# Cross-attention and expert FFN in one kernel: the experts' weights split on ScalarE and GpSimd, the context's LayerNorm applied on GpSimd, and new orders of work on all five engines

## Chip, cores and metric

One core of a Trainium2 chip. The metric is the device time of one execution in microseconds; the time before is the median of three runs. A span is the time from the first to the last instruction of the profiled execution.

## What is computed

Inputs: x (4, 512, 128), a context (4, 77, 96) with a mask of its valid positions, weights of one attention and of eight experts. All in float32.

```
ln   = layernorm(layernorm(x)) * g + b              # latents: 4 x 512 x 128
xn   = layernorm(ctx) * g + b                       # context: 4 x 77 x 96
q    = ln @ Wq.T
k, v = concat(xn @ Wkv.T, ln @ Wlkv.T)              # 77 + 512 keys, 2 heads of 64
attn = softmax(rmsnorm(q) * 64**-0.5 @ rmsnorm(k).T, masked context keys out)
x    = x + (attn @ v) @ Wo.T + bo
l2   = layernorm(x)
gates = softmax(l2 @ Wg + bg); top 2 of 8 experts
x    = x + sum over the two chosen e: gate[e] * (l2 @ W[e] + b[e])
```

## The kernel before

Each batch's 512 rows are four tiles of 128. The front (LayerNorm, q, k, v, their norms) runs over five parts p: batch 0 in two halves (parts 0 and 1), then batches 1, 2, 3 (parts 2, 3, 4). The rear (scores, exp, values, denominators, projection, second LayerNorm, gate, experts) runs over four parts, the batches. Per batch there are five groups of keys (four of 128, the context as the fifth): `score p n` is six matmuls for two heads, `exp p n` the exponentials on ScalarE, `value p n` the product with V. The sum of exponentials is formed by `e01` and `e23` on GpSimd (128x1024 each) and `esum` on VectorE, and `den` on TensorE reads it.

The scores and the experts are computed with rounded operands and their rests: a value is H (rounded to fp32r) plus L (the rest), and a product is H*H + H*L + L*H, three matmuls. WeH and WeL are the rounded experts' weights and their rest. They come from We0 = We_sb - We_end (`shifted`, GpSimd, L386), into whose last row the experts' biases are then loaded by two DMAs from SP that wait for `shifted` (L341, L342). In the kernel before, `split` on VectorE (L751 to L756) waits for these DMAs, makes WeH and then WeL.

An expert job is `low p n` or `high p n` (tile n of batch p, four experts each, 3 matmuls of 512 columns, L977 to L979). ScalarE scales the four low results (`low`, L685), GpSimd adds them up (`pair`, L478 and L479), VectorE accumulates the four high ones onto x for two tiles at a time (`high`, L932), and GpSimd adds both (`res`, L487), upon which SP stores two tiles. The last tile is different: ScalarE scales its high results too (L695), TensorE sums all eight (`sum`, L1213), VectorE adds them to x (`final`, L960) and SP stores the tile after all others. The last but one goes by `high1 3 2` on VectorE (L949), `pair1` and `res1` on GpSimd (L496, L497, L504).

The context's LayerNorm: `ctx_stats` on VectorE, `ctx_rstd` on GpSimd (a power, L413), `ctx_apply` on VectorE (four instructions of 77x96, L836, one per batch), `ctxT` on TensorE (L1071).

The order of the work is written out in four texts (TENSOR, VECTOR, SCALAR, GPSIMD) list the jobs of each engine as kind, part, number, and TENSOR adds the PSUM banks (of eight) of each job. `walk` issues the jobs of an engine in that order, each with its waits on semaphores. A job of TensorE also waits until the job that last had its banks has been read (`free`, with the table RELEASED). `warm p n` issues n transposes of the identity that nobody reads. So a wait of one job holds up all that stand behind it in its engine's text.

Of the kernel before, what the change touches and what calls it, by code (L numbers as in the profile page):

```python
# [5 lines left out]
ALU = mybir.AluOpType  # L6
ACT = mybir.ActivationFunctionType
AX = mybir.AxisListType
F32 = mybir.dt.float32
# [18 lines left out]
    warm 0 14 7   weights 0 0 0   warm 1 2 7   weights2 0 0 1   warm 2 4 7   xT 0 0 2   warm 3 4 7   k 0 0 3  # L28
    v 0 0 4   xT 1 0 5   q 0 0 6   ssk 0 0 7   k 1 0 0   ctxT 0 0 1   q 1 0 2   ssk 1 0 5   v 1 0 4   ctx_v 0 0 1
    ctx_k 0 0 7   maskT 0 0 5   xT 2 0 3   qT 0 0 0   ctx_ss 0 0 6   qT 1 0 5   v 2 0 2   q 2 0 3   k 2 0 7  # L30
    score 0 0 14   score 0 1 06   ssk 2 0 2   score 0 2 51   score 0 3 47   value 0 0 2   qT 2 0 0   value 0 1 -
    value 0 2 -   value 0 3 -   score 0 4 63   score 1 0 15   score 1 1 47   xT 3 0 0   value 0 4 -   value 1 0 3
    den 0 0 6   score 1 2 15   proj 0 0 47   score 1 3 20   v 3 0 6   q 3 0 1   k 3 0 5   denT 0 0 0
    score 1 4 26   value 1 1 -   value 1 2 -   value 1 3 -   value 1 4 -   xT 4 0 2   ssk 3 0 6   qT 3 0 0
    k 4 0 4   v 4 0 7   q 4 0 3   l2T 0 0 1   ssk 4 0 2   den 1 0 5   score 2 0 64   score 2 1 07   score 2 2 21
    gate 0 0 5   qT 4 0 4   denT 1 0 6   value 2 0 3   score 2 3 07   score 2 4 12   value 2 1 -   value 2 2 -
    value 2 3 -   value 2 4 -   proj 1 0 40   score 3 0 71   score 3 1 25   den 2 0 3   score 3 2 17
    score 3 3 04   score 3 4 62   proj 2 0 53   denT 2 0 1   value 3 0 7   value 3 1 -   value 3 2 -
    value 3 3 -   value 3 4 -   l2T 1 0 0   low 0 0 4   low 0 1 2   gate 1 0 6   den 3 0 1   proj 3 0 35
    denT 3 0 7   low 0 2 0   low 0 3 4   l2T 2 0 2   low 1 0 1   low 1 1 0   low 1 2 3   high 0 0 5   high 0 1 7  # L40
    high 0 2 4   high 0 3 6   high 1 0 1   high 1 1 0   high 1 2 3   gate 2 0 5   high 1 3 7   l2T 3 0 2
    low 1 3 4   low 2 0 6   gate 3 0 2   low 2 1 0   low 2 2 1   low 2 3 4   low 3 0 5   low 3 1 6   high 2 0 0
# [6 lines left out]
    ctx_kL 0 0   stats1 3 0   QL 0 0   ctx_ms 0 0   QL 1 0   stats1 4 0   ssq 2 0   kL 2 0   msk 2 0   qn 2 0
    QL 2 0   esum 0 0   split 0 0   ssq 3 0   x2 0 0   stats2 0 0   qn 3 0   kL 3 0   msk 3 0   esum 1 0   kL 4 0  # L50
    QL 3 0   ssq 4 0   msk 4 0   qn 4 0   logits 0 0   QL 4 0   top 0 0   esum 2 0   x2 1 0   stats2 1 0   x2 2 0
    stats2 2 0   esum 3 0   logits 1 0   x2 3 0   top 1 0   stats2 3 0   high 0 0   high 0 1   logits 2 0
    high 1 0   top 2 0   logits 3 0   high 1 1   top 3 0   high 2 0   high 2 1   high 3 0   high1 3 2   final 3 0
"""
SCALAR = """
    weights 0 0   apply1 0 0   weights2 0 0   lnT 0 0   apply1 1 0   k 0 0   lnT 1 0   qsq 0 0   v 0 0   k 1 0
    ctxT 0 0   qsq 1 0   apply1 2 0   ctx_k 0 0   lnT 2 0   QH 0 0   ctx_v 0 0   QH 1 0   v 1 0   v 2 0   qsq 2 0
    k 2 0   exp 0 0   exp 0 1   exp 0 2   exp 0 3   QH 2 0   apply1 3 0   exp 0 4   exp 1 0   exp 1 1   oT 0 0
    lnT 3 0   dens 0 0   exp 1 2   exp 1 3   v 3 0   qsq 3 0   apply1 4 0   exp 1 4   k 3 0   oT 1 0   lnT 4 0
    apply2 0 0   k 4 0   QH 3 0   qsq 4 0   v 4 0   l2T 0 0   dens 1 0   exp 2 0   exp 2 1   exp 2 2   QH 4 0  # L60
    exp 2 3   exp 2 4   gexp 0 0   oT 2 0   exp 3 0   exp 3 1   dens 2 0   exp 3 2   exp 3 3   exp 3 4
    apply2 1 0   oT 3 0   l2T 1 0   low 0 0   low 0 1   dens 3 0   apply2 2 0   gexp 1 0   low 0 2   low 0 3
    low 1 0   low 1 1   low 1 2   l2T 2 0   apply2 3 0   gexp 2 0   l2T 3 0   low 1 3   low 2 0   low 2 1
    gexp 3 0   low 2 2   low 2 3   low 3 0   low 3 1   low 3 2   low 3 3   high1 3 3
"""
GPSIMD = """
    blanks 0 0   ident 0 0   rstd1 0 0   rstd1 1 0   ctx_rstd 0 0   rstd1 2 0   rq 0 0   rk 0 0   rq 1 0
    xbo 0 0   xbo 1 0   rk 1 0   rstd1 3 0   ctx_rk 0 0   rq 2 0   e01 0 0   rk 2 0   e23 0 0   rstd1 4 0
    shifted 0 0   e01 1 0   e23 1 0   rq 3 0   xbo 2 0   rstd2 0 0   rk 3 0   rq 4 0   l2L 0 0   rk 4 0   e01 2 0
    e23 2 0   xbo 3 0   e01 3 0   rstd2 1 0   e23 3 0   rstd2 2 0   l2L 1 0   pair 0 0   pair 0 1   rstd2 3 0  # L70
    res 0 0   pair 1 0   l2L 2 0   res 0 1   l2L 3 0   res 1 0   pair 1 1   pair 2 0   res 1 1   pair 2 1
    res 2 0   pair 3 0   res 2 1   pair1 3 2   res 3 0   res1 3 2
# [1180 lines left out]
```

## Time and profile before

| | |
|---|---|
| median of 3 runs | 109.7 us (109.4 to 109.74) |
| profiled execution | 109.68 us, span 107.9 us |
| TensorE matmul busy | 100.8 us, 93% |
| ScalarE busy | 84.4 us, 78% |
| GpSimd busy | 81.6 us, 76% |
| VectorE busy | 69.9 us, 65% |
| granted TensorE clock | full in all 40 slices |
| DMA | 3.92 MB, nearly all in the first 20 us; the stores of the result begin at 85 us |

Busy shares are averages over stages. A matmul's end is modelled, so two matmuls can overlap in the profile and a short wait can lie under a modelled end: the distance between starts tells more. A timeline line merges neighbouring instructions of one kind: start, duration, engine, line, operation, output and inputs, shapes, count, and in brackets the idle time before it with what ended it.

### The profile page before, as it was taken

The numbers are of one execution on the slowest core, as the hardware profiler recorded it, in microseconds if no ns is written. First come the engines' busy times: TensorE is split into PE (matmuls) and PEld (weight loads), VectorE is DVE, ScalarE is ACT, GpSimd is POOL, SyncE is SP. The second block draws the span as 40 slices with busy tenths as digits, with TensorE's granted clock in tenths as the row PEclk, the third lists the DMA queues.
The fourth block names the chain that finished last, engine by engine and source line by source line (L and its number), as shares of the span: only waits on it lengthen the run. The fifth ranks groups of instructions, "written<-read, shape, count | busy, mean of one in ns | idle before, by whom it ended". The sixth has DMA issues, their size and how long they took to land. (4 is left out here: it accounts for less than half of the span.)

```text
span 107.9 us, 2374 instructions
## 1 busy us (share of the span) xinstructions
PE 100.8 (93%) x687; PEld 69.9 (65%) x687; DVE 69.9 (65%) x324; ACT 84.4 (78%) x198; POOL 81.6 (76%) x85
## 2 busy tenths in 40 slices
PE   2999999999999999999999999999999989999950
PEld 2978877753537842897843668346888867868730
DVE  0658889732131769944461792992598989979950
ACT  0479888999698997897998299969989929697910
POOL 4337799979999197864996229988729698999990
PEclk9999999999999999999999999999999999999999
DMA  3734875000000000000000000000000001101113
GB/s 79 215 79 130 241 192 71 10 0 3 0 0 8 0 0 0 0 0 6 3 0 0 0 9 0 0 0 0 9 0 0 18 31 49 52 0 55 49 49 97
DMA packets 6823, 3.92 MB, mean 36 GB/s; under 512 B 2330, under 2 KB 6426, under 8 KB 6811
## 3 DMA queue, kind: packets, MB, share of 16 engines
q1 hardware_dynamic: 5979, 3.41, 11.8%
q10 hardware_dynamic: 832, 0.36, 1.2%
q8 instruction: 6, 0.10, 0.4%
q14 instruction: 6, 0.05, 0.2%
HBM read 2.72 MB, written 1.05 MB: 35 GB/s over the span
## 5 line engine op out<-in xcount | busy, mean ns | idle before, releaser
L627 ACT ACTIVATE probs<-PS,shift,rk 128x512 f32<-128x512 f32 x32 | 22.3, 786 | 2.7 <-PE PS L1110 2.6
L685 ACT ACTIVATE scaled<-PS,w 128x128 f32<-128x128 f32 x64 | 17.5, 390 | 2.4 <-POOL low L479 1.6
L1131 PE MATMUL PS<-probs,V_sb 128*64 128x512 f32 x64 | 15.3, 603 | 0.1
L977 PE MATMUL PS<-WeH,l2H 128*128 128x512 f32 x32 | 13.2, 413 | 0.4 <-issue 0.3
L979 PE MATMUL PS<-WeH,l2L 128*128 128x512 f32 x32 | 12.5, 391 | 0.0
L978 PE MATMUL PS<-WeL,l2H 128*128 128x512 f32 x32 | 12.5, 391 | 0.0
L435 POOL TENSOR_TENSOR e<-probs,probs 128x1024 f32<-128x1024 f32 x4 | 9.5, 2374 | 3.2 <-ACT probs L627 3.2
L478 POOL TENSOR_TENSOR pair<-scaled 128x512 f32<-128x512 f32 x7 | 9.0, 1288 | 3.4 <-ACT scaled L685 2.8
L426 POOL TENSOR_TENSOR esum<-probs,probs 128x1024 f32<-128x1024 f32 x4 | 9.5, 2370 | 0.6 <-ACT probs L627 0.6
L401 POOL TENSOR_TENSOR rq<-msq,half 128x8 f32<-128x8 f32 (+1 forms) x5 | 6.9, 1387 | 2.9 <-DVE msq L779 2.9
L1131 PEld LDWEIGHTS PS<-probs,V_sb 128*64 128x64 f32 x64 | 4.0, 136 | 7.7 <-issue 6.7
L447 POOL TENSOR_TENSOR xbo<-x_sb,bo_b 128x512 f32<-128x512 f32 x4 | 5.1, 1296 | 4.7 <-DVE x L869 4.7
L407 POOL TENSOR_TENSOR rk<-msk,half 128x8 f32<-128x8 f32 (+1 forms) x5 | 7.9, 1573 | 0.1
L932 DVE SCALAR_TENSOR_TENSOR part<-PS,w,part 128x128 f32<-128x128 f32 x28 | 7.8, 341 | 0.0
L977 PEld LDWEIGHTS PS<-WeH,l2H 128*128 128x128 f32 x32 | 6.0, 188 | 2.2 <-issue 0.7
L1110 PE MATMUL PS<-QH,KH 64*128 64x512 f32 x32 | 7.1, 437 | 0.0
L979 PEld LDWEIGHTS PS<-WeH,l2L 128*128 128x128 f32 x32 | 6.0, 188 | 1.3
L986 PE MATMUL PS<-ident 128*128 128x128 f32 x24 | 4.8, 361 | 2.1 <-POOL ident L371 2.1
L850 DVE TENSOR_TENSOR esum<-esum,e 128x1024 f32<-128x1024 f32 x4 | 4.9, 1222 | 2.9 <-POOL e L435 2.9
L654 ACT ACTIVATE l<-x,nm,rstd 128x127 f32<-128x127 f32 x16 | 6.6, 494 | 0.2 <-POOL nm L456 0.2
L536 ACT ACTIVATE xh<-x_sb,nm,rstd 128x128 f32<-128x128 f32 x16 | 6.7, 497 | 0.0
L978 PEld LDWEIGHTS PS<-WeL,l2H 128*128 128x128 f32 x32 | 6.0, 189 | 1.0
(161 smaller groups left out, 258.3 us busy)
## 6 DMA issues: line engine op xcount, KB each, us to landing
out_dram<-x SPq DMA_DIRECT2D x7, 128.0 KB, 1.7
x_sb<-in_x_dram SPq DMA_DIRECT2D x3, 256.0 KB, 4.1
We_sb<-in_L_ffn_W_dram SPq DMA_DIRECT2D x1, 512.0 KB, 5.5
We_end<-in_L_ffn_W_dram SPq DMA_DIRECT2D x1, 512.0 KB, 9.3
x_sb<-in_x_dram SPq DMA_DIRECT2D x2, 128.0 KB, 2.5
Wlkv_sb<-in_L_xattn_Wlkv_dram ACTq DMA_DIRECT2D x1, 128.0 KB, 3.0
out_dram<-x SPq DMA_DIRECT2D x2, 64.0 KB, 1.7
ctx_sb<-in_ctx_dram SPq DMA_DIRECT2D x1, 115.5 KB
```

What stands on the lines that cost most here:

```text
L407: pool.tensor_tensor(rk[:, b, a:e], msk[:, b, a:e], half[:, 0:H * (e - a)].rearrange("p (t h) -> p t h", h=H), ALU.pow).then_inc(rk_made, 1)
L426: pool.tensor_tensor(esum[p % 2][:, :, s], probs[p % 2][0][:, :, s], probs[p % 2][1][:, :, s], ALU.add).then_inc(e01_made, 1)
L435: pool.tensor_tensor(e23[:, :, s], probs[p % 2][2][:, :, s], probs[p % 2][3][:, :, s], ALU.add).then_inc(e23_made, 1)
L478: step(pool.tensor_tensor(pair[:], scaled[m % 2][:, :, 0:EH // 2], scaled[m % 2][:, :, EH // 2:EH], ALU.add))
L627: act.activation(probs[p % 2][n][:, h, s], ps[:, s], ACT.Exp, bias=shift[:, 0:1], scale=rk[:, b, n, h:h + 1]).then_inc(probs_made, 1)
L685: last = act.activation(scaled[m // 2 % 2][:, m % 2, e], ps[:, e], ACT.Copy, scale=w[:, m, e:e + 1])
L932: last = dve.scalar_tensor_tensor(dst, bank("high", p, 2 * n + k)[:, e * C:(e + 1) * C], w[:, m, EH + e:EH + e + 1], src, ALU.mult, ALU.add)
L977: pe.matmul(dst, lH, rH, start=True, stop=False)
L978: pe.matmul(dst, lH, rL, start=False, stop=False)
L979: return pe.matmul(dst, lL, rH, start=False, stop=True)
L1110: last = pe.matmul(bank("score", p, n, h)[0:P if n < T else M, 0:(e - a) * P], k, queries[r, b % 2, a * P:e * P], start=(step == 0), stop= ...
L1131: last = pe.matmul(bank("value", p, 0)[h * D:(h + 1) * D, s], v, pr, start=(n == 0), stop=(n == KT - 1))
```

## The change

`split` leaves VectorE: WeH is now made by a copy on ScalarE, WeL by a subtraction on GpSimd that waits for WeH. The four context applies leave VectorE and follow the power on GpSimd; their separate semaphore is gone. All four written orders are new; the jobs in them are the same but for these and for the warm transposes (24 in four jobs before, 25 in six after).

```diff
+            def WeL_(p, n):
+                pool.wait_ge(WeH_made, 1)
+                pool.tensor_tensor(WeL[:], We0[:], WeH[:].bitcast(F32), ALU.subtract).then_inc(WeL_made, 1)
...
             def ctx_rstd_(p, n):
                 pool.wait_ge(cmv_made, 1)
                 pool.wait_ge(half_made, 1)
-                pool.tensor_tensor(crstd[:], cvar[:], half[0:M, 0:B], ALU.pow).then_inc(crstd_made, 1)
+                step(pool.tensor_tensor(crstd[:], cvar[:], half[0:M, 0:B], ALU.pow))
+                for b in range(B):
+                    last = pool.tensor_scalar(cxh[:, b], ctx_sb[:, b], cmv[:, b, 0:1], crstd[:, b:b + 1], ALU.subtract, ALU.mult)
+                last.then_inc(cxh_made, 1)
...
+            def WeH_(p, n):
+                act.wait_ge(biases_in, 32)
+                act.copy(WeH[:], We0[:]).then_inc(WeH_made, 1)
...
-            def split_(p, n):
-                dve.wait_ge(biases_in, 32)
-                dve.tensor_copy(WeH[:], We0[:]).then_inc(WeH_made, 1)
-                dve.wait_ge(WeH_made, 1)
-                dve.tensor_tensor(WeL[:], We0[:], WeH[:].bitcast(F32), ALU.subtract).then_inc(WeL_made, 1)
...
-            def ctx_apply_(p, n):
-                dve.wait_ge(crstd_made, 1)
-                for b in range(B):
-                    last = dve.tensor_scalar(cxh[:, b], ctx_sb[:, b], cmv[:, b, 0:1], crstd[:, b:b + 1],
-                                             ALU.subtract, ALU.mult)
-                last.then_inc(cxh_made, 1)
```

The parts of the new orders that matter below (kind, part, number, and banks in TENSOR):

```
TENSOR   warm 0 14 7  weights 0 0 0  warm 1 2 7  weights2 0 0 1  warm 2 4 7  xT 0 0 2  warm 3 2 7  xT 1 0 3
         warm 4 1 7  v 0 0 4  q 0 0 5  k 0 0 6  q 1 0 7  ctxT 0 0 0  v 1 0 2  ssk 0 0 1  maskT 0 0 3
         ctx_v 0 0 6  ctx_k 0 0 0  qT 0 0 1  xT 2 0 5  qT 1 0 3  ctx_ss 0 0 6  q 2 0 7  v 2 0 5  k 1 0 6
         k 2 0 1  warm 5 2 4  ssk 1 0 4  score 0 0 25  score 0 1 36  score 0 2 40  ssk 2 0 1  qT 2 0 7
         value 0 0 2  score 0 3 51  score 0 4 36  ...
         value 1 4 -  den 1 0 1  q 3 0 7  q 4 0 4  k 3 0 5  denT 1 0 0  k 4 0 3  v 3 0 6  ssk 3 0 2  v 4 0 1
         qT 3 0 5  ssk 4 0 7  qT 4 0 2  l2T 0 0 6  proj 1 0 43  score 2 0 15  ...
         high 1 3 4  l2T 3 0 5  low 2 0 6  low 2 1 2  gate 3 0 3  low 2 2 7  low 2 3 1
         high 2 0 5  high 2 1 6  low 3 0 0  low 3 1 4  high 2 2 2  high 2 3 7  high 3 0 3  low 3 2 1
         low 3 3 5  high 3 1 6  high 3 2 0  high 3 3 4  sum 3 0 2  sum 3 1 -
VECTOR   ... QL 2 0  esum 0 0  esum 1 0  x2 0 0  stats2 0 0  ssq 3 0  ssq 4 0  kL 3 0  qn 3 0  msk 3 0 ...
SCALAR   weights 0 0  apply1 0 0  apply1 1 0  lnT 0 0  weights2 0 0  lnT 1 0  qsq 0 0  k 0 0  qsq 1 0
         ctxT 0 0  apply1 2 0  ctx_v 0 0  ctx_k 0 0  lnT 2 0  QH 0 0  QH 1 0  v 0 0  v 1 0  qsq 2 0  v 2 0
         k 1 0  k 2 0  apply1 3 0  exp 0 0 ...  apply1 4 0  exp 1 4  WeH 0 0  lnT 3 0  oT 1 0  lnT 4 0 ...
GPSIMD   ... ctx_rstd 0 0  rstd1 2 0  rq 0 0  rq 1 0  rk 0 0  xbo 0 0  xbo 1 0  ctx_rk 0 0  rstd1 3 0
         rq 2 0  rk 1 0  shifted 0 0  rk 2 0  e01 0 0  e23 0 0  rstd1 4 0  e01 1 0  e23 1 0  WeL 0 0
         xbo 2 0  rstd2 0 0  rq 3 0  rq 4 0  rk 3 0  rk 4 0  l2L 0 0  xbo 3 0  ...
         pair 0 0  res 0 0  pair 0 1  rstd2 3 0  pair 1 0  res 0 1  l2L 2 0  res 1 0  pair 1 1  l2L 3 0
         res 1 1  pair 2 0  pair 2 1  res 2 0  pair 3 0  res 2 1  pair1 3 2  res 3 0  res1 3 2
```

## Rows read from the trace of the kernel before

**Rows 1.** Windows: from:to, length; busy us of PE, PEld, DVE, ACT, POOL; clock, DMA share, GB/s.

```profile
8.40:18.92 10.52, 10.49 (x80) 8.82 (x80) 9.12 (x49) 9.47 (x24) 9.28 (x11) 1.00 0.65 162
18.92:50.13 31.21, 31.13 (x231) 18.74 (x231) 16.71 (x46) 28.26 (x51) 25.05 (x18) 1.00 0.01 2
50.13:101.60 51.47, 50.95 (x335) 35.22 (x331) 37.75 (x194) 42.00 (x113) 40.29 (x36) 1.00 0.04 14
83.90:105.40 21.50, 19.47 (x99) 15.29 (x97) 18.63 (x93) 14.88 (x50) 19.08 (x22) 1.00 0.11 38
```

**Rows 2.** Timeline of TensorE, value jobs, then expert jobs at two waits.

```profile
39.80 2.79 PE L1131 MATMUL PS<-probs,V_sb 128*64 128x512 f32 x12
...
88.17 0.40 PE L979 MATMUL PS<-WeH,l2L 128*128 128x512 f32 x1
...
88.86 0.47 PE L977 MATMUL PS<-WeH,l2H 128*128 128x512 f32 x1 [0.30 <-issue]
...
94.32 0.39 PE L977 MATMUL PS<-WeH,l2H 128*128 128x512 f32 x1
...
94.77 0.39 PE L979 MATMUL PS<-WeH,l2L 128*128 128x512 f32 x1
95.25 0.50 PE L977 MATMUL PS<-WeH,l2H 128*128 128x512 f32 x1
```

**Rows 3.** Timeline at the end: TensorE, VectorE, GpSimd, SP's queue.

```profile
101.60 1.13 PE L1213 MATMUL PS<-scaled,ident 128*128 128x128 f32 x8
...
104.18 0.29 DVE L960 TENSOR_TENSOR x<-PS,x 128x128 f32<-128x128 f32 x1 [0.48 <-PE PS L1213]
...
104.88 0.46 POOL L504 TENSOR_TENSOR x<-low,acc 128x128 f32<-128x128 f32 x1
...
105.80 0.45 SPq L354 DMA_DIRECT2D out_dram<-x  x1
```

**Rows 4.** Timeline of VectorE, what the change takes away.

```profile
9.27 1.04 DVE L836 TENSOR_SCALAR cxh<-ctx_sb,cmv,crstd 77x96 f32<-77x96 f32 x4
...
34.65 1.30 DVE L754 CAST WeH<-We 128x1024 fp32r<-128x1024 f32 x1 [4.12 <-DMA Wg<-in_L_ffn_bg_dram]
35.98 1.23 DVE L756 TENSOR_TENSOR WeL<-We,WeH 128x1024 fp32r<-128x1024 f32 x1
```

**Rows 5.** Timelines, prices of the nearest operations, GpSimd's and one of ScalarE.

```profile
1.80 0.29 POOL L371 TENSOR_SCALAR_AFFINE_SELECT ident<-ident 128x128 f32<-128x128 f32 x1 [0.24 <-POOL ident L369]
...
7.98 1.00 POOL L413 TENSOR_TENSOR crstd<-cvar,half 77x4 f32<-77x4 f32 x1 [1.66 <-DVE cvar L831]
...
30.54 2.36 POOL L386 TENSOR_TENSOR We<-We_sb,We_end 128x1024 f32<-128x1024 f32 x1
...
103.78 0.45 POOL L497 TENSOR_TENSOR low<-pair 128x128 f32<-128x128 f32 x1
...
19.52 0.58 ACT L582 CAST KH<-PS 128x512 fp32r<-128x512 f32 x1
```

**Rows 6.** Timelines, eight exps on ScalarE, and a pair and the job after it on GpSimd.

```profile
20.00 5.47 ACT L627 ACTIVATE probs<-PS,shift,rk 128x512 f32<-128x512 f32 x8
...
94.07 1.29 POOL L478 TENSOR_TENSOR pair<-scaled 128x512 f32<-128x512 f32 x1
...
96.13 0.74 POOL L487 TENSOR_TENSOR x<-low,acc 128x256 f32<-128x256 f32 x1
```

**Rows 7.** Timelines where GpSimd and VectorE read SBUF at once.

```profile
29.14 1.03 POOL L394 TENSOR_TENSOR rstd<-var,half 128x4 f32<-128x4 f32 x1
...
29.30 1.23 DVE L850 TENSOR_TENSOR esum<-esum,e 128x1024 f32<-128x1024 f32 x1 [2.47 <-POOL e L435]
...
44.95 1.22 DVE L850 TENSOR_TENSOR esum<-esum,e 128x1024 f32<-128x1024 f32 x1
...
45.12 2.55 POOL L407 TENSOR_TENSOR rk<-msk,half 128x8 f32<-128x8 f32 x1
...
49.90 1.64 POOL L401 TENSOR_TENSOR rq<-msq,half 128x8 f32<-128x8 f32 x1 [2.23 <-DVE msq L779]
```

More of the change, by code:

```diff
@@ L27 @@
 TENSOR = """
[L28 to L42, printed above, removed]
@@ L43 @@
-    high 2 1 1   high 2 2 3   high 2 3 7   low 3 2 2   low 3 3 4   high 3 0 5   high 3 1 0   high 3 2 1
-    high 3 3 6   sum 3 0 2   sum 3 1 -
+    warm 0 14 7   weights 0 0 0   warm 1 2 7   weights2 0 0 1   warm 2 4 7   xT 0 0 2   warm 3 2 7   xT 1 0 3
+    warm 4 1 7   v 0 0 4   q 0 0 5   k 0 0 6   q 1 0 7   ctxT 0 0 0   v 1 0 2   ssk 0 0 1   maskT 0 0 3
+    ctx_v 0 0 6   ctx_k 0 0 0   qT 0 0 1   xT 2 0 5   qT 1 0 3   ctx_ss 0 0 6   q 2 0 7   v 2 0 5   k 1 0 6
+    k 2 0 1   warm 5 2 4   ssk 1 0 4   score 0 0 25   score 0 1 36   score 0 2 40   ssk 2 0 1   qT 2 0 7
@@ new lines @@
+    value 0 0 2   score 0 3 51   score 0 4 36   value 0 1 -   value 0 2 -   score 1 0 04   score 1 1 71
+    value 0 3 -   value 0 4 -   value 1 0 5   score 1 2 36   score 1 3 04   score 1 4 17   den 0 0 2
+    proj 0 0 36   value 1 1 -   value 1 2 -   value 1 3 -   denT 0 0 0   xT 3 0 4   xT 4 0 2   value 1 4 -
+    den 1 0 1   q 3 0 7   q 4 0 4   k 3 0 5   denT 1 0 0   k 4 0 3   v 3 0 6   ssk 3 0 2   v 4 0 1   qT 3 0 5
+    ssk 4 0 7   qT 4 0 2   l2T 0 0 6   proj 1 0 43   score 2 0 15   score 2 1 72   gate 0 0 6   score 2 2 15
@@ new lines @@
+    score 2 3 03   score 2 4 42   value 2 0 7   value 2 1 -   value 2 2 -   value 2 3 -   value 2 4 -
+    score 3 0 15   score 3 1 03   proj 2 0 24   score 3 2 67   value 3 0 1   den 2 0 5   score 3 3 03
+    score 3 4 67   denT 2 0 5   value 3 1 -   value 3 2 -   value 3 3 -   value 3 4 -   high 0 0 0   high 0 1 3
+    l2T 1 0 6   low 0 0 7   low 0 1 2   gate 1 0 4   den 3 0 5   proj 3 0 16   denT 3 0 0   low 0 2 3   low 0 3 7
+    l2T 2 0 2   high 0 2 5   high 0 3 4   low 1 0 3   low 1 1 0   gate 2 0 1   low 1 2 6   low 1 3 7   high 1 0 2
@@ L45 @@
+    high 1 1 3   high 1 2 0   high 1 3 4   l2T 3 0 5   low 2 0 6   low 2 1 2   gate 3 0 3   low 2 2 7   low 2 3 1
+    high 2 0 5   high 2 1 6   low 3 0 0   low 3 1 4   high 2 2 2   high 2 3 7   high 3 0 3   low 3 2 1
+    low 3 3 5   high 3 1 6   high 3 2 0   high 3 3 4   sum 3 0 2   sum 3 1 -
 """
 VECTOR = """
-    consts 0 0   stats1 0 0   stats1 1 0   ln_gain 0 0   ctx_stats 0 0   stats1 2 0   ctx_apply 0 0   gain 0 0
-    ssq 0 0   shift 0 0   mask 0 0   msk 0 0   msk 1 0   ssq 1 0   kL 0 0   kL 1 0   qn 0 0   cbias 0 0   qn 1 0
@@ L49 @@
[L49 to L53, printed above, removed]
+    consts 0 0   stats1 0 0   stats1 1 0   ln_gain 0 0   ctx_stats 0 0   stats1 2 0   gain 0 0   ssq 0 0   kL 0 0
@@ new lines @@
+    mask 0 0   ssq 1 0   msk 0 0   shift 0 0   qn 0 0   cbias 0 0   qn 1 0   stats1 3 0   ctx_ms 0 0   QL 0 0
+    stats1 4 0   ssq 2 0   QL 1 0   kL 1 0   msk 1 0   ctx_kL 0 0   kL 2 0   qn 2 0   msk 2 0   QL 2 0   esum 0 0
+    esum 1 0   x2 0 0   stats2 0 0   ssq 3 0   ssq 4 0   kL 3 0   qn 3 0   msk 3 0   qn 4 0   kL 4 0   QL 3 0
+    msk 4 0   QL 4 0   x2 1 0   logits 0 0   stats2 1 0   top 0 0   esum 2 0   x2 2 0   stats2 2 0   esum 3 0
+    high 0 0   logits 1 0   top 1 0   x2 3 0   stats2 3 0   high 0 1   logits 2 0   high 1 0   top 2 0   high 1 1
@@ L54 @@
+    logits 3 0   top 3 0   high 2 0   high 2 1   high 3 0   high1 3 2   final 3 0
 """
 SCALAR = """
[L56 to L64, printed above, removed]
+    weights 0 0   apply1 0 0   apply1 1 0   lnT 0 0   weights2 0 0   lnT 1 0   qsq 0 0   k 0 0   qsq 1 0
@@ new lines @@
+    ctxT 0 0   apply1 2 0   ctx_v 0 0   ctx_k 0 0   lnT 2 0   QH 0 0   QH 1 0   v 0 0   v 1 0   qsq 2 0   v 2 0
+    k 1 0   k 2 0   apply1 3 0   exp 0 0   exp 0 1   exp 0 2   QH 2 0   exp 0 3   exp 0 4   exp 1 0   exp 1 1
+    oT 0 0   exp 1 2   exp 1 3   dens 0 0   apply1 4 0   exp 1 4   WeH 0 0   lnT 3 0   oT 1 0   lnT 4 0
+    dens 1 0   qsq 3 0   qsq 4 0   k 3 0   apply2 0 0   k 4 0   v 3 0   QH 3 0   v 4 0   QH 4 0   l2T 0 0
+    exp 2 0   exp 2 1   exp 2 2   exp 2 3   exp 2 4   gexp 0 0   apply2 1 0   oT 2 0   exp 3 0   exp 3 1
@@ L65 @@
+    exp 3 2   dens 2 0   exp 3 3   exp 3 4   oT 3 0   l2T 1 0   low 0 0   low 0 1   dens 3 0   gexp 1 0
+    apply2 2 0   low 0 2   low 0 3   l2T 2 0   low 1 0   low 1 1   low 1 2   apply2 3 0   gexp 2 0   low 1 3
+    l2T 3 0   low 2 0   low 2 1   low 2 2   gexp 3 0   low 2 3   low 3 0   low 3 1   low 3 2   low 3 3
+    high1 3 3
 """
 GPSIMD = """
-    blanks 0 0   ident 0 0   rstd1 0 0   rstd1 1 0   ctx_rstd 0 0   rstd1 2 0   rq 0 0   rk 0 0   rq 1 0
-    xbo 0 0   xbo 1 0   rk 1 0   rstd1 3 0   ctx_rk 0 0   rq 2 0   e01 0 0   rk 2 0   e23 0 0   rstd1 4 0
@@ L69 @@
[L69 to L72, printed above, removed]
+    blanks 0 0   ident 0 0   rstd1 0 0   rstd1 1 0   ctx_rstd 0 0   rstd1 2 0   rq 0 0   rq 1 0   rk 0 0
@@ new lines @@
+    xbo 0 0   xbo 1 0   ctx_rk 0 0   rstd1 3 0   rq 2 0   rk 1 0   shifted 0 0   rk 2 0   e01 0 0   e23 0 0
+    rstd1 4 0   e01 1 0   e23 1 0   WeL 0 0   xbo 2 0   rstd2 0 0   rq 3 0   rq 4 0   rk 3 0   rk 4 0   l2L 0 0
+    xbo 3 0   e01 2 0   rstd2 1 0   e23 2 0   e01 3 0   e23 3 0   rstd2 2 0   l2L 1 0   pair 0 0   res 0 0
+    pair 0 1   rstd2 3 0   pair 1 0   res 0 1   l2L 2 0   res 1 0   pair 1 1   l2L 3 0   res 1 1   pair 2 0
+    pair 2 1   res 2 0   pair 3 0   res 2 1   pair1 3 2   res 3 0   res1 3 2
@@ L253, in build @@
             sem("Wlat_done"), sem("Wctx_done"), sem("WT_made"), sem("WoT_made"), sem("WctxT_made"), sem("WeH_made"), sem("WeL_made"))
-        cmv_made, crstd_made, cxh_made, ctxT_done, cT_made, ck_done, ck_made, cv_done, cv_made, css_done, cms_made, crk_made = (
-            sem("cmv_made"), sem("crstd_made"), sem("cxh_made"), sem("ctxT_done"), sem("cT_made"), sem("ck_done"), sem("ck_made"),
+        cmv_made, cxh_made, ctxT_done, cT_made, ck_done, ck_made, cv_done, cv_made, css_done, cms_made, crk_made = (
+            sem("cmv_made"), sem("cxh_made"), sem("ctxT_done"), sem("cT_made"), sem("ck_done"), sem("ck_made"),
             sem("cv_done"), sem("cv_made"), sem("css_done"), sem("cms_made"), sem("crk_made"))
@@ L505, in res1_ @@
                                    ALU.add).then_inc(res_made, 1)
-            walk(GPSIMD, dict(pair1=pair1_, res1=res1_, ident=ident_, blanks=blanks_, shifted=shifted_, rstd1=rstd1_, rq=rq_, rk=rk_, ctx_rstd=ctx_rstd_, ctx_rk=ctx_rk_,
+            walk(GPSIMD, dict(pair1=pair1_, res1=res1_, ident=ident_, blanks=blanks_, shifted=shifted_, WeL=WeL_, rstd1=rstd1_, rq=rq_, rk=rk_, ctx_rstd=ctx_rstd_, ctx_rk=ctx_rk_,
                               e01=e01_, e23=e23_, xbo=xbo_, rstd2=rstd2_, l2L=l2L_, pair=pair_, res=res_))
@@ L696, in high1_ @@
                 last.then_inc(high_scaled, 1)
-            walk(SCALAR, dict(high1=high1_, apply2=apply2_, apply1=apply1_, weights=weights_, weights2=weights2_, lnT=lnT_, qsq=qsq_, QH=QH_, k=k_, v=v_, ctxT=ctxT_, ctx_k=ctx_k_,
+            walk(SCALAR, dict(high1=high1_, apply2=apply2_, WeH=WeH_, apply1=apply1_, weights=weights_, weights2=weights2_, lnT=lnT_, qsq=qsq_, QH=QH_, k=k_, v=v_, ctxT=ctxT_, ctx_k=ctx_k_,
                               ctx_v=ctx_v_, exp=exp_, dens=dens_, oT=oT_, l2T=l2T_, gexp=gexp_, low=low_))
@@ L960, in final_ @@
                 dve.tensor_tensor(x2[:, B - 1, T - 1], bank("sum", p, 0)[:, 0:C], x2[:, B - 1, T - 1], ALU.add).then_inc(final_made, 1)
-            walk(VECTOR, dict(high1=high1_, final=final_, consts=consts_, ln_gain=ln_gain_, gain=gain_, shift=shift_, mask=mask_, cbias=cbias_, split=split_, stats1=stats1_,
-                              ssq=ssq_, qn=qn_, kL=kL_, QL=QL_, ctx_kL=ctx_kL_, msk=msk_, ctx_stats=ctx_stats_, ctx_apply=ctx_apply_,
+            walk(VECTOR, dict(high1=high1_, final=final_, consts=consts_, ln_gain=ln_gain_, gain=gain_, shift=shift_, mask=mask_, cbias=cbias_, stats1=stats1_,
+                              ssq=ssq_, qn=qn_, kL=kL_, QL=QL_, ctx_kL=ctx_kL_, msk=msk_, ctx_stats=ctx_stats_,
                               ctx_ms=ctx_ms_, esum=esum_, x2=x2_, stats2=stats2_,
```

## The prediction

> **What bounds the kernel now.** I read the windows first, cut at the first score (18.92 us), at batch 2's first score (50.13) and at the end of the expert matmuls. TensorE is busy for all but 0.6 us of the 93 us from 8.40 to 101.60, at a granted clock of 1.00, while the others have 10 to 50% to spare [rows 1]. Busy there includes short waits that a modelled matmul end covers, so I went on to TensorE's timeline and compared starts. An expert job (three 128x512 matmuls) takes 0.68 us (94.32 to 94.77 is two steps of 0.23, and the third follows), but the job after it starts at 95.25 instead of 95.00, and the one of 88.17 is followed at 88.86 instead of 88.40 [rows 2]. So two waits of 0.25 and 0.46 us stand in the rear, in sum 0.7. Third I read the end: matmuls of the experts stop at 101.60, the last VectorE instruction ends at 104.47, GpSimd's last ends at 105.34, and then SP issues two stores one after the other and the second lands at 107.9 [rows 3]. The result of `final` is ready 0.87 us before GpSimd's, and its store must queue behind that of GpSimd's tile. GpSimd is busy for 19.08 of 21.50 us before the end [rows 1]: it is the second bound, in the tail alone.
>
> So the time is: the start of real matmul work, plus a fixed amount of TensorE work, plus its waits, plus a tail of 6.3 us (101.60 to 107.9). The span is 107.9 in an execution of 109.68, thus 1.8 us lie around it; the median of the runs is 109.7, the same.
>
> **What the change removes.** VectorE loses four 77x96 applies, 1.04 us, and the rounding and rest of the experts' weights, 1.30 + 1.23 us [rows 4]. VectorE is busy 3.5 us less, and I put none of it into the sum by itself: its share is 54% in the middle stretch [rows 1], and the rounding ran at 34.65 with half of that stretch's VectorE free. What it gives is freedom for the orders.
>
> **What it adds.** ScalarE rounds 1024 columns: the 512-column cast took 0.58 [rows 5], so from 0.9 (one fixed part for both halves) to 1.3 (VectorE's own time [rows 4]); I take 1.1. GpSimd forms the rest: the same shape and operation as `shifted`, 2.36 us [rows 5]; bounds 2.3 and 3.6 (2.36 plus one VectorE 1.23 it may have to sit out). GpSimd applies the context's LayerNorm in four instructions of 77x96 with one tensor input. No such row exists here. Nearest below is the 128x128 one-input select, 0.29; nearest above the 128x128 two-input add, 0.45 [rows 5]; farther above is the power on 77x4, 1.00. I take 0.32, by the one-input row, so 1.3 us; ends 0.8 (twice as fast as the select, a quarter smaller) and 4.0.
>
> Where these lie. The context apply follows the power that ends at 8.98 [rows 5], so it ends at 10.4 plus a handover, against 10.31 on VectorE [rows 4]. The new order puts ctxT behind v, q, k of part 0 and q of part 1, which I place at 10.4: about 0.1 us of wait. Behind it on GpSimd stands rstd1 of part 2, then both rq: part 2's apply on ScalarE starts at about 11.8, xT 2 is due on TensorE at 13.6, so it is covered; at 4.0 us it isn't. The rounding on ScalarE stands after exp 1 4 and before lnT 3, which xT 3 and q 3 don't need before 41 us; exps take 0.68 each [rows 6] and I place it at 38.3 to 39.3. The rest on GpSimd follows e23 of batch 1; its first reader is high 0 0, at about 71: 30 us of cover. What it pushes on is xbo 2, rstd2 0, rq 3, rq 4, rk 3, rk 4: they end at about 51, each 0.5 us or more ahead of its reader (qn 3 for qT 3 is the tightest: 47.4 against 47.9). The DMAs of the biases wait for `shifted`, which moves ahead of rk 2 and e01 0, from 30.5 to about 22.7; they land long before 38.
>
> The Trainium skill speaks against the move: first the row, 2.36 us on GpSimd against 1.23 on VectorE for 1024 columns with two inputs [rows 4, 5], a ratio of 1.9; the GPSIMD Engine Reference, section 4.1, says elementwise work belongs on VectorE, GpSimd being about twice as slow with two inputs and roughly as fast with one. By its one-input rule the four applies would cost what VectorE took, 1.04 instead of my 1.3, and the sum would be the same, since the wait at ctxT is 0.1 us.
>
> **The new orders, replayed.** I put every job of the four orders one after the other with the durations of the rows (an expert or score job 0.69, a value job 0.93 [rows 2], an exp 0.68 and a pair on GpSimd, 94.07 to 96.13, 2.06 [rows 6]) and looked at each job's semaphores and freed bank. The work of TensorE is the same but for one warm transpose more, about 0.2 us.
>
> Front: v 0 starts at 8.55 (ScalarE now does both applies first) with xT 1 already behind it; waits of 0.25 before the context's sums and 0.2 before q 2 appear, the two last warm transposes fill 0.4 where there is real work to do, and a wait of about 0.2 for a K is gone. The first score comes at 19.5 instead of 18.92: +0.55.
> Middle: before, batch 2's first score comes 31.21 us later [rows 1]. Pricing its jobs without waits gives 30.3 and 0.2 of overhead, so 0.7 of small waits were in it (value 0 4, ssk 2, v 3 and others). In the new order I find each input ready by 0.1 to 3 us; I give back a third for what a hand replay misses: -0.5. (exp 0 0 starts 1.7 us later than before, and value 0 0 comes just then, at 23.1; this is the tightest point.)
> Rear: the two waits of 0.7 and about 0.2 at a gate go; a new one of 0.35 comes at low 2 0, for l2L 2, which stands on GpSimd behind pair 1 0 and res 0 1. -0.55.
> Tail: high 2 0 and high 2 1 now stand ahead of low 3 0, so VectorE has them while it waited before, and GpSimd has pair 0 1 and res 0 0 done before rstd2 3. GpSimd's chain from there is 19.5 us long and ends at 104.3 at the latest, against 105.34. TensorE's experts end at 101.1, `final` 2.9 later at 104.0; the stores then end at about 104.3 + 0.5 + 2.1 = 106.9. That is 5.8 behind TensorE's end instead of 6.3: -0.5.
> Sum: 0.55 - 0.5 - 0.55 - 0.5 = -1.0, minus 0.1 for GpSimd's earlier start, taken as **-1.1: 108.6 us** (span 106.8). Its own range is 108.0 to 109.3.
>
> **Rivals.**
> *A: the waits only move.* The new order has as many short waits as the old one (0.7 in the middle, 0.9 in the rear), because they are unseen in a replay. Then +0.55 in front, nothing in the middle and rear, -0.5 in the tail: 109.7, range 109.4 to 110.0. For it: the replay of the old order shows some waits only in hindsight. Against it: those in the rear are tied to named jobs, which have moved.
> *B, slower: the weights' rest holds up esum 1.* On rows: GpSimd's rk began at 45.12 while VectorE's esum (two SBUF inputs) ran until 46.17, and took 2.55 us where the like took 1.64: it sat out 0.9 [rows 7]. The other way round, an esum begun at 29.30 took its usual 1.23 although a power on 4 columns was under way on GpSimd from 29.14 to 30.17 [rows 7]; no row has esum against a large add. If a large GpSimd add blocks as it was blocked, and ScalarE has the rounding ready before e23 1 ends, the rest starts at once, some 0.1 us ahead of esum 1, which then starts 2.3 us late; den 1 on TensorE finds it at 42.5 instead of 40.4: +2.1, for 108.6 + 2.1 = 110.7. It decides where the rounding ends before e23 1 does; I have 39.3 against 38.9, close.
> The Trainium skill, page "SBUF — State Buffer", section "SBUF: two separate sides", says that the pair shared by VectorE and GpSimd is locked for the whole instruction by whichever starts first. By that rule, the trace agrees at rk and not at the esum of 29.30.
> *C: the context apply is dear.* At 1.00 each (the power's price), ctxT waits till 13.1 and everything behind it: +2.6, 111.2. Break-even with the time before is at about 0.6 each. Against it: no arithmetic without power costs over 0.45 here at such a size.
> *D: more than I sum.* The new order has no wait of its own (-0.8 more): 107.8.
>
> **How the numbers follow.** Forecast 0.54, A 0.19, B 0.12, C 0.06, D 0.09. A difference of 0.3% (0.33 us) is about what can be told from none. Faster: the forecast but for a sliver, and D, and a little of A: 0.66. Same: most of A: 0.15. Slower: B, C, a rest of A: 0.19. The range takes D's end down to 107.6, and reaches up to 110.5, short of B's centre; what is outside is C, half of B and a part of D, under 0.2.
>
> **What would show it.** Right: the first score at 19.3 to 19.7; batch 2's first score some 31 to 32 us later (it now has qT 4, denT 1 and proj 1, 1.6 us of work, ahead of it, so at about 51.7); expert matmuls ended at 100.7 to 101.3; the last GpSimd add ended by 104.3; applies on GpSimd of 0.25 to 0.45. Wrong: a wait on TensorE before den 1 or ctxT over 0.5 us, an esum over 1.5 us, applies over 0.6, exps that start after TensorE needs value 0 0, or a GpSimd that is still adding pairs 4 us behind the last expert matmul.

## Result: slower by 0.4%, where 1.0% faster was forecast

| | before | changed |
|---|---|---|
| median of 20 runs | 109.7 us | 110.12 us |
| ratio, 95% interval | | 1.0038, 1.0024 to 1.0053 |
| span of the profiled execution | 107.9 us | 108.3 us |

The forecast was 108.6 us, with a range of 107.6 to 110.5. The time lies in the range, but on the other side of the time before. The ratios leave out the few executions that ran longer at a lower granted clock (one of the 20 here, 112.55 us at 0.964), while the medians count them.

I cut the changed kernel at the same three events as [rows 1]: first score, batch 2's first score, end of the expert matmuls. Columns as there.

```profile
8.23:20.16 11.93, 10.48 (x80) 9.06 (x79) 9.12 (x49) 9.59 (x25) 11.75 (x14) 1.00 0.59 145
20.16:53.05 32.89, 32.76 (x253) 20.29 (x254) 15.07 (x40) 29.46 (x54) 28.80 (x21) 1.00 0.01 2
53.05:102.56 49.51, 48.98 (x315) 33.93 (x312) 36.57 (x193) 41.38 (x111) 38.58 (x36) 1.00 0.05 15
```

The middle holds 1.69 us of TensorE work (qT 4, denT 1, proj 1, by the distances between their starts in the kernel before) that came later before, so its 32.89 stands against 31.21 + 1.69 = 32.90, and the 49.51 of the rear against 51.47 - 1.69 = 49.78. Front: the first score comes at 20.16 instead of 18.92. So: front +1.24, middle 0, rear -0.27, tail (102.56 to 108.3 against 101.60 to 107.9) -0.56, in sum +0.4. In the front row TensorE is busy 10.48 of 11.93 us while GpSimd is busy for 11.75: the first stretch has a new bound. TensorE's timeline of the changed kernel shows where it meets this bound (`ctxT` is L1071), and a second wait in the rear:

```profile
9.66 0.61 PE L1027 MATMUL PS<-WT,lnT 128*128 128x128 f32 x4
11.68 0.44 PE L1071 MATMUL PS<-ident,cxh 77*96 77x77 f32 x4 [1.42 <-POOL cxh L421]
...
14.50 0.38 PE L1064 MATMUL PS<-ident,qn 128*128 128x128 f32 x2
...
89.51 0.60 PE L1181 MATMUL PS<-ident,l 128*128 128x128 f32 x4
90.63 0.47 PE L977 MATMUL PS<-WeH,l2H 128*128 128x512 f32 x1 [0.53 <-ACT scaled L699]
```

ctxT waits 1.42 us for the context applies. The second wait is the one I had placed at low 2 0: the profile names ScalarE, but l2L 2 on GpSimd (L474) ends at 90.53, just before. GpSimd in the front, around the weights' rest, and at l2L 2:

```profile
7.70 1.00 POOL L419 TENSOR_TENSOR crstd<-cvar,half 77x4 f32<-77x4 f32 x1 [1.41 <-DVE cvar L838]
8.81 2.73 POOL L421 TENSOR_SCALAR cxh<-ctx_sb,cmv,crstd 77x96 f32<-77x96 f32 x4
11.51 1.02 POOL L400 TENSOR_TENSOR rstd<-var,half 128x4 f32<-128x4 f32 x1
...
36.98 2.37 POOL L444 TENSOR_TENSOR e<-probs,probs 128x1024 f32<-128x1024 f32 x1 [0.85 <-ACT probs L641]
41.04 2.40 POOL L393 TENSOR_TENSOR WeL<-We,WeH 128x1024 fp32r<-128x1024 f32 x1 [1.69 <-ACT WeH L541]
...
89.25 1.28 POOL L474 TENSOR_TENSOR l2L<-l2T,l2H 128x512 fp32r<-128x512 f32 x1
```

The four applies take 2.73 us, 0.68 each, where VectorE took 1.04 for all four [rows 4]. The rest of the weights took 2.40, as forecast. Its companions, VectorE's esum 1 and ScalarE's rounding:

```profile
39.45 1.22 DVE L850 TENSOR_TENSOR esum<-esum,e 128x1024 f32<-128x1024 f32 x1 [5.72 <-POOL e L444]
...
39.91 1.06 ACT L541 CAST WeH<-We 128x1024 fp32r<-128x1024 f32 x1
```

And the end, to be laid beside [rows 3]:

```profile
102.56 1.05 PE L1213 MATMUL PS<-scaled,ident 128*128 128x128 f32 x8
...
105.22 0.29 DVE L960 TENSOR_TENSOR x<-PS,x 128x128 f32<-128x128 f32 x1 [0.51 <-PE PS L1213]
...
105.27 0.45 POOL L513 TENSOR_TENSOR x<-low,acc 128x128 f32<-128x128 f32 x1
...
106.19 0.45 SPq L355 DMA_DIRECT2D out_dram<-x  x1
```

GpSimd's last add now ends 3.2 us after the expert matmuls' end (105.72), not 3.7, and VectorE's final at 105.51 is nearly level.

### The profile page after: what moved, and what is told of

The parts are those of the page before. It is cut to its first block and busy times, and to the rows that moved or that the text cites. A ratio compares the mean times of both kernels' runs of the same rounds, so it can differ in the third digit from the quotient of the medians.

```text
span 108.3 us, 2377 instructions
## 1 busy us (share of the span) xinstructions
PE 100.2 (93%) x688; PEld 70.1 (65%) x688; DVE 67.2 (62%) x318; ACT 85.4 (79%) x199; POOL 85.6 (79%) x90
## 3 DMA queue, kind: packets, MB, share of 16 engines
HBM read 2.72 MB, written 1.05 MB: 35 GB/s over the span
## 5 line engine op out<-in xcount | busy, mean ns | idle before, releaser
L413 POOL TENSOR_TENSOR rk<-msk,half 128x8 f32<-128x8 f32 (+1 forms) x5 | 6.9, 1386 | 1.1 <-DVE msk L802 1.1
L464 POOL TENSOR_TENSOR rstd<-var,half 128x4 f32<-128x4 f32 x4 | 5.0, 1251 | 2.0 <-DVE var L884 2.0
```

## Experiments

All but the ruler were timed over several executions; each ratio is to the kernel before, run beside it on the same chip. The diffs are shortened.

**1. Applies back on VectorE.** The rest of the changed kernel stays.

```diff
 GPSIMD ctx_rstd: -  four pool.tensor_scalar(cxh ...)      (power alone, signals crstd_made)
 VECTOR: - stats1 2 0   gain 0 0
         + stats1 2 0   ctx_apply 0 0   gain 0 0
```

> The changed kernel with one part undone: the four context applies are back on VectorE (after stats1 2), with their own semaphore; every other job and order as in the changed kernel. Theory 1 (the applies are dear on GpSimd, 0.68 us each where 0.32 was taken, and TensorE waits 1.42 us for them at ctxT, which is never made good): the wait at ctxT falls under 0.2 us, the first score comes at 18.8 to 19.0 instead of 20.16, and the time is 1.1 to 1.4 us below the changed kernel's 110.1, so 108.7 to 109.0, faster than the kernel before by 0.6 to 0.9%. Theory 2 (the new orders meet as many waits as the old, whoever applies): the first score comes earlier, but the next limit takes the gain back before the end; the time is 109.4 or more.

108.46 us, ratio 0.9879 (0.9853 to 0.9906). TensorE in its front, with at most 0.15 us of wait at ctxT, by the starts, and the first score at 18.70:

```profile
10.34 0.44 PE L1075 MATMUL PS<-ident,cxh 77*96 77x77 f32 x4
...
13.16 0.38 PE L1068 MATMUL PS<-ident,qn 128*128 128x128 f32 x2
...
18.70 0.50 PE L1114 MATMUL PS<-QH,KH 64*128 64x512 f32 x2
```

Theory 1 holds, a little more than it said: 1.66 us come back. Batch 2's first score stands at 51.26 and the expert matmuls end at 100.71, so against the kernel before the front is 0.22 us shorter, the middle 0.34, the rear 0.33, and the tail, now 5.7, 0.6 shorter.

**2. Weights' part back on VectorE, applies still on GpSimd.**

```diff
 SCALAR:  - exp 1 4 0   WeH 0 0   lnT 3 0      + exp 1 4 0   lnT 3 0
 GPSIMD:  - e23 1 0   WeL 0 0   xbo 2 0        + e23 1 0   xbo 2 0
 VECTOR:  - esum 0 0   esum 1 0                + esum 0 0   split 0 0   esum 1 0
```

> The changed kernel with the other part undone: WeH and WeL are made on VectorE again (split, after esum 0), nothing of them on ScalarE or GpSimd. VectorE has nothing to do from 33.7 to 39.4 us, so split (2.5 us) fits in. Theory 1 (the weights' part hardly touches the time, the applies do): within 0.2 us of the changed kernel, 109.9 to 110.3; lnT 3 on ScalarE may start 1 us earlier, TensorE needs it only at 43.4. Theory 2 (the added 1.06 us on ScalarE and 2.4 us on GpSimd cost time in the middle, where 0.5 us of the forecast gain is missing): batch 2's first score comes 0.3 to 0.6 us earlier than 53.05 and the time falls to 109.5 to 109.8.

110.29 us, 1.0046 (1.0023 to 1.0069): no different from the changed kernel (1.0038). Theory 2 falls.

**3. The new orders alone**, experiments 1 and 2 together.

> The new orders alone: both applies and split are on VectorE as in the kernel before (apply after stats1 2, split after esum 0), all the rest in the changed kernel's orders. Theory 1: as with the applies alone undone, 108.7 to 109.0, so the orders are worth 0.7 to 1.0 us, and moving the work off VectorE is worth nothing or less. Theory 2 (the orders only work because VectorE was freed): slower than with the applies alone undone by 0.3 us or more.

108.44 us, 0.9884 (0.9859 to 0.9909), the same as experiment 1. All of the gain is the orders'; freeing VectorE of the weights is worth nothing that can be measured, whether the applies are on GpSimd (experiment 2) or on VectorE (experiment 3).

**4. The applies on GpSimd alone**, in the kernel before and its orders, run twice.

```diff
 GPSIMD ctx_rstd: +  four pool.tensor_scalar(cxh ...)
 VECTOR: - stats1 2 0   ctx_apply 0 0   gain 0 0
         + stats1 2 0   gain 0 0
```

> The kernel before with one part of the change alone: the four applies follow the power on GpSimd, orders as before. Theory 1: they take 2.7 us from 9.0 on, are done at 11.8 instead of 10.3, ctxT on TensorE (due at 10.97) waits about 0.9 us, and rstd1 of part 2 and both rq behind them come 2 us later; the first score comes 0.9 to 1.6 us later and the time is 110.5 to 111.2. Theory 2 (the applies are slow only in the company of the new order's VectorE work): they take 0.3 to 0.45 each here and the time stays within 0.3 us of 109.7.

> The order of before with the applies on GpSimd once more, for a second profile. In the first one TensorE began its real work 0.4 us later than in the kernel before, so that the applies were ready in time (11.26 against a ctxT at 11.40), and nothing of the price was to be seen, while its median over the runs was 0.5 us above the kernel before. Theory 1 (the price shows where TensorE is early): with k 0 at 8.4 or so ctxT waits 0.2 to 0.6 us, and the time is about 110.3 again. Theory 2: no wait and a time within 0.2 of 109.7.

110.28 us, 1.0043 (1.0024 to 1.0062), and 110.06 us, 1.0036 (1.0015 to 1.0056). Theory 1 of the first had the sign and the price of the applies right (2.71 for four), but the time came out under its 110.5 to 111.2, and in that profile ctxT did not wait: TensorE began its real work only at 8.81, and the applies were ready at 11.26 for a ctxT at 11.40. In the second profile TensorE begins at 8.17, and ctxT waits. GpSimd's row first:

```profile
8.80 2.70 POOL L415 TENSOR_SCALAR cxh<-ctx_sb,cmv,crstd 77x96 f32<-77x96 f32 x4
...
11.65 0.44 PE L1067 MATMUL PS<-ident,cxh 77*96 77x77 f32 x4 [0.74 <-POOL cxh L415]
...
19.34 0.50 PE L1106 MATMUL PS<-QH,KH 64*128 64x512 f32 x2
```

In both, the first score stands at 19.3, 0.4 us behind the profile of the kernel before, and the medians say the same (0.5 and 0.3 us). The old order puts ssk 0 and k 1 ahead of ctxT, the new one only q 1, and the old one transposes q's first half at 15.0, the new one, when nothing holds it up, at 13.2 (experiment 1). So the old order pays 0.4 at the first score for what costs the new one 1.5. That this distance to the readers makes the difference is argued from the rows; no run moves these jobs alone.

**5. Applies on both engines.** VectorE makes what ctxT reads; GpSimd does the same work into an unused tile.

```diff
 (as experiment 1, and in GPSIMD's ctx_rstd, behind the power:)
+ for b in range(B):
+     pool.tensor_scalar(cxh_idle[:, b], ctx_sb[:, b], cmv[:, b, 0:1], crstd[:, b:b + 1], ALU.subtract, ALU.mult)
```

> As the kernel with the applies back on VectorE (108.5), but GpSimd still does the four applies too, into a tile that nobody reads: ctxT gets its input at 10.3, while GpSimd's queue is as long as in the changed kernel. Theory 1a (the loss is the wait at ctxT itself): 108.4 to 108.7, the wait is gone and the first score stays at 18.7 to 18.9. Theory 1b (the loss is what queues on GpSimd behind the applies: rstd1 of part 2 and both rq come at 12.8 to 14.7 instead of 10.6 to 12.8): TensorE now waits before qT 0 and xT 2, due at 13.2 and 13.4, for about 1.0 us; the first score comes at 19.7 to 20.1 and the time is 109.4 to 110.0.

110.19 us, 1.0039 (1.0007 to 1.0071): theory 1b, at a time 0.2 above its range. ctxT runs at 10.16 without a wait, and yet no time is gained that these runs can tell; a wait now stands at qT 0 (L1072), for q's norms, which are behind the applies in GpSimd's queue:

```profile
12.47 0.68 PE L1086 MATMUL PS<-cT,WctxT 96*128 96x308 f32 x2
14.05 0.41 PE L1072 MATMUL PS<-ident,qn 128*128 128x128 f32 x2 [0.89 <-DVE qn L795]
...
19.84 0.50 PE L1118 MATMUL PS<-QH,KH 64*128 64x512 f32 x2
```

So the wait at ctxT was only the first place where TensorE met GpSimd's longer queue. In the profiles the first score comes at 20.16 in the changed kernel, 19.84 here and 18.70 in experiment 1: of the 1.46 us, 1.14 stay although ctxT no longer waits. Had I gone by the row "waited 1.42 us for cxh" alone, I would have moved ctxT back and, by this run, won little or nothing.

**6. A cheaper form on GpSimd.** The changed kernel, with two wide instructions for the four.

```diff
-  for b in range(B):
-      last = pool.tensor_scalar(cxh[:, b], ctx_sb[:, b], cmv[:, b, 0:1], crstd[:, b:b + 1], ALU.subtract, ALU.mult)
-  last.then_inc(cxh_made, 1)
+  step(pool.tensor_tensor(cxh[:], ctx_sb[:], cmv[:, :, 0:1].to_broadcast([M, B, CX]), ALU.subtract))
+  pool.tensor_tensor(cxh[:], cxh[:], crstd[:].unsqueeze(2).to_broadcast([M, B, CX]), ALU.mult).then_inc(cxh_made, 1)
```

> The changed kernel, where GpSimd applies by two tensor_tensor over all four batches (77x384, mean and rstd broadcast along the columns) instead of four tensor_scalar with two pointers. Theory 1 (the price per element of the form with pointers is what is dear, 0.68 us for 96 columns): from the two-input rows (0.45 at 128 columns, 1.29 at 512) 384 columns cost 1.0 each, 2.1 in all instead of 2.73, so ctxT comes 0.6 us earlier and the time is 109.5 to 109.8. Theory 2 (GpSimd is as slow with any form here, because it shares SBUF with VectorE's statistics at that moment): 2.7 us or more, the time 110.0 to 110.4.

109.07 us, 0.9949 (0.9932 to 0.9966), better than theory 1 had it, since the instructions are cheaper than the rows gave:

```profile
9.06 0.83 POOL L420 TENSOR_TENSOR cxh<-ctx_sb,cmv 77x384 f32<-77x384 f32 x1
9.97 0.82 POOL L421 TENSOR_TENSOR cxh<-cxh,crstd 77x384 f32<-77x384 f32 x1
```

1.7 us instead of 2.7, and 1.05 us less time: this microsecond on GpSimd was one of the whole. It does not go on so: taking the remaining 1.7 us off GpSimd too (experiment 1) gives only another 0.6, and there GpSimd waits 0.45 and 0.25 us for VectorE's results before rstd1 and rq 0. With GpSimd still applying, the changed kernel is now faster than the one before.

**7. The ruler.** Forms of the apply behind the changed kernel's last work on GpSimd, run once; only the durations of the rows are of interest.

> The changed kernel with ten more GpSimd instructions at its end, when VectorE is done or nearly so; they write to tiles that are dead by then. Only their durations are of interest: tensor_scalar 77x96 with two pointers (twice) and 77x384, the same with two constants (96 and 384), one pointer (96 and 384), one constant (96), and tensor_tensor 77x96 plain and with a broadcast scalar column. Theory 1 (the form is dear by itself): two pointers cost 0.6 to 0.7 again at 96 columns, and the constants much less, about 0.3. Theory 2 (contention with VectorE at 9 to 11 us made them dear): two pointers cost 0.3 to 0.45 here.

```profile
108.22 0.69 POOL L520 TENSOR_SCALAR We_sb<-ctx_sb,cmv,crstd 77x96 f32<-77x96 f32 x1
...
109.57 1.64 POOL L522 TENSOR_SCALAR We_sb<-ctx_sb,cmv,crstd 77x384 f32<-77x384 f32 x1
111.18 0.53 POOL L523 TENSOR_SCALAR We_sb<-ctx_sb 77x96 f32<-77x96 f32 x1
...
113.17 0.53 POOL L525 TENSOR_SCALAR We_sb<-ctx_sb,crstd 77x96 f32<-77x96 f32 x1
...
114.90 0.44 POOL L527 TENSOR_SCALAR We_sb<-ctx_sb 77x96 f32<-77x96 f32 x1
115.31 0.38 POOL L528 TENSOR_TENSOR We_sb<-ctx_sb 77x96 f32<-77x96 f32 x1
```

Top to bottom: two pointers (96 and 384 columns), two constants, one pointer, one constant, a product of two tensors. A pointer here is a scalar that is read from a tile, one per partition. Theory 1 holds for the pointers: the form is dear by itself, since VectorE's last instruction had ended at 108.01, and VectorE's company as the cause falls. It was wrong on the constants, which cost 0.53 and not 0.3: the second operation costs 0.09, the two pointers 0.16 more, and even the form with one constant is dearer than a product of two tensors.

**8. The wait at low 2 0 removed** from experiment 1's kernel.

```diff
 GPSIMD: - pair 1 0   res 0 1   l2L 2 0   res 1 0
         + pair 1 0   l2L 2 0   res 0 1   res 1 0
```

> The kernel with the applies back on VectorE, and on GpSimd l2L 2 stands ahead of res 0 1 instead of behind it. TensorE waits at low 2 0, 88.08 to 88.81 in that kernel, for l2L 2, which ends 0.1 us before. Theory 1 (this wait is a loss of the new order that lasts to the end): l2L 2 ends 0.7 us earlier, the expert matmuls end 0.5 to 0.7 us earlier, and the time falls from 108.46 to 107.8 to 108.1. Theory 2 (ScalarE's l2T 3 or GpSimd's tail is next, or the chain on GpSimd sets the end): less than 0.2 us.

108.4 us, 0.9877 (0.9844 to 0.9909): theory 2. The expert matmuls do end 0.5 us earlier, but GpSimd's last add ends as before, so the tail is 6.3 us again instead of 5.7. First this kernel, then experiment 1's:

```profile
100.19 1.13 PE L1217 MATMUL PS<-scaled,ident 128*128 128x128 f32 x8
...
103.48 0.45 POOL L510 TENSOR_TENSOR x<-low,acc 128x128 f32<-128x128 f32 x1
```

```profile
100.71 1.05 PE L1217 MATMUL PS<-scaled,ident 128*128 128x128 f32 x8
...
103.42 0.45 POOL L510 TENSOR_TENSOR x<-low,acc 128x128 f32<-128x128 f32 x1
```

**9. One job of GpSimd's tail moved to VectorE**, on top of experiment 8.

```diff
 GPSIMD: - l2L 3 0   res 1 1   pair 2 0      + l2L 3 0   pair 2 0
 VECTOR: - logits 3 0   top 3 0              + logits 3 0   res 1 1   top 3 0
```

> The kernel with the applies on VectorE and l2L 2 earlier, and one job of GpSimd's tail, res 1 1 (128x256, 0.74 us there), moved to VectorE between logits 3 and top 3. In the kernel without this move the expert matmuls ended 0.5 us earlier than before l2L 2 was moved, but the last GpSimd add still ended at 103.9 and the time stayed at 108.4. Theory 1 (GpSimd's chain, back to back from 84 us on, sets the end): its last add ends 0.6 to 0.7 us earlier, at about 103.2, where VectorE's final (103.0) is as late; the time falls by 0.3 to 0.6 us, to 107.8 to 108.1. Theory 2 (VectorE is as near to the end: it takes 0.4 us more in front of top 3 and of everything behind it, and its accumulations feed GpSimd): no change, 108.3 to 108.5, with waits of GpSimd for VectorE in the tail.

107.89 us, 0.983 (0.9804 to 0.9855), the best kernel here; the interval just meets that of experiment 8, whose lower end is 0.9844. Theory 1: GpSimd's chain sets the end. In the profiles its last add starts at 103.15 instead of 103.48, though this one is already 0.18 us later at GpSimd's pair of 81 us (81.29 against 81.11); from that pair to the last add the chain is 0.51 us shorter, which is what the medians give. Of the 0.74 us moved, 0.2 is lost on GpSimd's next instruction, which ran beside VectorE's (1.48 where the like takes 1.29):

```profile
92.64 0.56 DVE L967 TENSOR_TENSOR x<-low,acc 128x256 f32<-128x256 f32 x1
...
92.88 1.48 POOL L484 TENSOR_TENSOR pair<-scaled 128x512 f32<-128x512 f32 x1
```

## Why the prediction was wrong, step by step

**The bounds of the kernel** were read rightly: TensorE throughout, GpSimd in the tail. Experiments 8 and 9 show the second, which before was argued. They also show that the rear and the tail were not two terms to be added, as my sum did: 0.5 us taken from the rear came back in the tail.

**The step that failed is the price of the context apply**: "I take 0.32, by the one-input row, so 1.3 us". It is 0.68 each and 2.73 in all, 1.4 us more than the term in my sum. I priced it by an instruction that makes no arithmetic on two pointers, and took the two-input add of 128 columns (0.45) as the nearest above; the ruler and experiment 6 show that at 96 and at 384 columns GpSimd's tensor_scalar costs more than its tensor_tensor. The Trainium skill, GPSIMD Engine Reference, section 4.1, which I quoted for one input at roughly VectorE's rate, does not hold for this form: 0.68 against 0.26 on VectorE is worse than its factor for two inputs. My range of 0.8 to 4.0 held it, and rival C had the mechanism, with a break-even at 0.6 each; at 0.68 the loss by C's reckoning is 1.42 less 0.1 at ctxT, 109.9, near what was measured. Experiment 6 agrees: at its 1.65 us, an estimate by my sum with only this term changed is 108.95, and 109.07 was measured. The low end of my range for the applies, 0.8, does not follow from the select that I named for it (twice as fast would be some 0.6 at most for four); nothing came of it. I gave C 0.06, because "no arithmetic without power costs over 0.45": an absence of rows, taken for a bound.

**The second part of that step** is the cover. I wrote that part 2's apply is "covered" by xT 2 at 13.6 and looked at ctxT as the place of the cost. Experiment 5 shows that ctxT was not the only place: rstd1 and both rq behind the applies come 1.6 to 1.9 us later than in experiment 1, TensorE waits 0.89 us at qT 0 instead of 1.42 at ctxT, and the time stays. C too had put the whole loss at ctxT, so its agreement in the number is in part luck.

**The new orders** are worth what I said and more: forecast -1.1 with cheap applies, measured -1.3 (experiments 1 and 3; 108.5 against my 108.6). That this is so close is in part luck, for the parts were less exact. Front: forecast +0.55, in experiment 1 -0.22. Of these 0.77 us, 0.23 is v 0, which starts at 8.32 and not 8.55, and about 0.1 the waits before q 2 and the context's sums, 0.16 each by the starts; the rest I can't place. Middle -0.5 against -0.34, rear -0.55 against -0.33, tail -0.5 against -0.6. In the changed kernel itself the middle brought 0, and the third of a microsecond went before value 0 0. GpSimd's longer queue shows there again, in rq 2, for which qT 2 waits, and in rstd1 3, for which the apply ahead of the exponentials waits: from the first score to value 0 0 are 4.08 us there (20.16 to 24.24) and 3.75 with the applies on VectorE (18.70 to 22.45).

**The weights' part at nothing** was right (experiments 2 and 3), with 1.06 us on ScalarE and 2.40 on GpSimd for the forecast 1.1 and 2.36.

**Rival A** fell: the waits did not merely move. **Rival B** did not come to pass, as the rounding ended at 40.97, after e23 1 (39.35), so that esum 1 started at 39.45 undisturbed, as the rows above show. But its mechanism exists: see below. **The wait at low 2 0** was foreseen at 0.35 us and is about 0.7; it makes the rear come out short of its forecast, but it cost nothing in the whole, since GpSimd's chain in the tail is as long (experiment 8). I had counted it as 0.35 of loss.

## To carry to other kernels

When a helper engine takes over a job, price it in the exact form (operation, kind of operands, columns), and where no row has that form, measure it or keep the far end of its range as a real case. A job added to a queue also costs where the queue's later products are wanted, not only where its own product is; the test is to keep the job and take away its reader. In a kernel whose longest engine never rests, ask the same of the second: ending TensorE's experts 0.5 us earlier gave nothing until GpSimd's chain was cut.
